# A transformer stack with cross-attention: heads in 32 rows of TensorE, and keys by way of DRAM

## The chip, the cores and the metric

One core of a Trainium2 chip runs the whole program as one launch. The metric is the device time of one execution in microseconds, as the median of several executions. TensorE multiplies, VectorE, ScalarE and GpSimd work elementwise, and SyncE issues the DMAs.

## The reference, cut to what matters

Eight layers work on `x`, 32 batches of 100 queries of 128 values, and each adds its gated result to `x`: attention, feed-forward, four times over. Three of the attention layers (called a0, a1 and a3 here) have 16 heads of 8 values and look at 1444 context rows of each batch:

```
q = layernorm(x) @ Wq;  k = ctx @ Wk;  v = ctx @ Wv           # per head: 8 of 128 columns
s = q @ k.T * scale                                           # 100 x 1444 for each of 16 heads
a1: s masked by a 0/1 mask [32, 100, 1444];  a3: keys from lens[b] on get -1.0e6
x += gate * (softmax(s) @ v) @ Wo
```

The fourth attention layer and the feed-forward layers are other functions.

## The kernel before, in words

`attention_phase` (line 195) is called three times: for a0, with a mask for a1 and with lengths for a3. Each call is one block in which five engines run their own lists of instructions and meet at semaphores. A batch's 16 heads are two halves of 8; the keys come in 12 tiles of 128 for scores and in 3 chunks of 480 or 482 for maxima. A batch is 24 units (`UNITS`). A unit has two maximum matmuls (`max_mm`, line 838), the scores of one half against one tile of 128 keys (`score_mm`, line 853), one exponential (`exps`, line 538), and its share of the product with the values (`pv_mm`, line 871), which is issued for two units together after each even unit. Maxima run ahead of scores by `LEAD` = 16 units, since a half's scores need its maxima.

Float32 accuracy is made from parts rounded to `F32R`: keys and queries are split into a high and a low part, and the three products high by high, low by high and high by low are rows of one matmul. For this `stack` (line 221) holds, for each group of four heads, 96 rows of keys (high, low, high, copied by twelve DMAs per batch in `stack_load`, line 373) and 32 rows of ones; `qblk` (line 225) holds, for each head, 96 query rows, zero outside of the head's own 8 (`q_spread`, line 439, on GpSimd), and 32 rows that carry the negated maxima (`neg_turn` on TensorE, `neg_copy` on VectorE, `neg_spread` on GpSimd). A maximum matmul therefore has 96 rows, 100 output rows and 480 or 482 columns. A score matmul has 128 rows, a stationary tile of 128 keys and 400 columns (four heads by 100 queries); two make a unit.

The maxima go through a ring of three PSUM banks (`RING`, line 191): `ring` (line 787) lets TensorE write a bank when what was in it three turns ago has been read. VectorE reduces each (`reduce_max`, line 649, with `tensor_reduce` in a0, and with a multiply or add of the mask or penalty in a1 and a3). The ring also takes each batch's other small products (`q_proj`, `u_proj`, `neg_turn`, `out_turn`, `concat_turn`, `out_proj`). Scores go through two slots of two banks (`slot`, line 792), which ScalarE empties; the projections `k_proj` and `v_proj` take the same slots. Which unit of a batch issues which of these is written out by hand in the constants of lines 295 to 297 and in the loop from line 925:

```
max_mm(2 * g)
score_mm(b, u)
# out_turn, concat_turn, out_proj, neg_turn, u_proj, q_proj at their units
max_mm(2 * g + 1)
# at even u: pv_mm of the two units before; then v_proj, k_proj at their units
```

In a1 `score_mm` adds a bf16 penalty matmul (line 867) to each of its two, and in a3 the penalty is the bias of the exponential (line 548).

## Time and profile before

| | us |
|---|---|
| median of 3 runs | 6736.84 (6734.98 to 6741.63) |
| profiled execution, its own time | 6736.52 |
| its span in the trace | 6734.7 |
| loop over batches in a0 (first to last score) | 1283.2, from 94.5 |
| loop over batches in a1 | 1718.3, from 2141.7 |
| loop over batches in a3 | 1351.6, from 5292.6 |
| TensorE, VectorE, ScalarE, GpSimd busy | 5947.1, 4732.6, 3471.3, 1972.7 |
| mean granted clock of TensorE | 0.938 |

The three loops are 4353.1 us of the span. Busy times of an engine merge instructions that overlap. A matmul of the trace lasts from its issue to its modelled end, so that many overlap; what one costs in a stream is the step from start to start. PE is TensorE's matmuls, PEld its loads of stationary operands, DVE is VectorE, ACT ScalarE, POOL GpSimd, SPq the DMA queue of SyncE.

### The profile page before, as it was taken

To read this page: it belongs to the slowest core of one execution; us is meant where nothing else is said; L and a number is where in the kernel's file an instruction comes from. 1 tells how busy PE (TensorE), PEld (TensorE's weight loads), DVE (VectorE), ACT (ScalarE), POOL (GpSimd) and SP (SyncE) were. 2 spreads that over 40 slices of the span, in tenths; PEclk is the share of its full clock that TensorE was granted. 3 is DMA by queue.
4 is the path that set the end of the run, shared out by engine and by line. 5 is a ranking of instruction groups with operands and counts; after the bars stand their busy time and mean duration, and the time that the engine had idled before them with its cause. 6 is when DMAs were issued, how large, how long until landed. Compare 5 with 4: busy or idle time off the path is not lost. (4 is left out here: it accounts for less than half of the span.)

```text
span 6734.7 us, 123692 instructions
## 1 busy us (share of the span) xinstructions
PE 5947.1 (88%) x42776; PEld 4044.1 (60%) x42776; DVE 4732.6 (70%) x12652; ACT 3471.3 (52%) x5250; POOL 1972.7 (29%) x1415
## 2 busy tenths in 40 slices
PE   6999999969897999999999956768498799999996
PEld 4666666659894555555555545645388466566653
DVE  6878777867676666666666676634577777777775
ACT  3666666655553444444444433423255466666664
POOL 2222222224453222222222122334255222222220
PEclk9999999989997999999999977878699799999998
DMA  3333333220002333333333132356332333232321
GB/s 75 77 78 73 72 72 75 63 68 21 21 21 68 81 77 81 78 79 75 76 79 75 35 68 52 60 157 183 98 118 81 82 72 71 67 69 68 69 67 25
DMA packets 200964, 492.88 MB, mean 73 GB/s; under 512 B 31689, under 2 KB 135318, under 8 KB 199162
## 3 DMA queue, kind: packets, MB, share of 16 engines
q1 hardware_dynamic: 200386, 485.47, 29.5%
q8 instruction: 327, 5.36, 0.3%
q14 instruction: 251, 2.06, 0.1%
HBM read 270.18 MB, written 2.25 MB: 40 GB/s over the span
## 5 line engine op out<-in xcount | busy, mean ns | idle before, releaser
L850 PE MATMUL a_max<-a_stack,a_qblk 96*100 96x482 f32 (+1 forms) x4608 | 2003.5, 455 | 114.3 <-DVE a_mx L671 35.7
L550 ACT ACTIVATE a_probs<-a_scores 128x800 f32<-128x800 f32 (+1 forms) x1536 | 1281.3, 838 | 1019.0 <-PE a_scores L867 656.9
L863 PE MATMUL a_scores<-a_qblk,a_stack 128*128 128x400 f32 (+1 forms) x4608 | 1378.7, 372 | 8.1 <-POOL a_qblk L455 2.7
L665 DVE CUSTOM_DVE_ANT_0 a_dump<-a_max,a_mqf 100x482 f32<-100x482 f32 (+1 forms) x1536 | 978.5, 657 | 426.4 <-PE a_max L850 395.6
L850 PEld LDWEIGHTS a_max<-a_stack,a_qblk 96*100 96x100 f32 x4608 | 767.2, 167 | 745.1 <-issue 205.6
L671 DVE CUSTOM_DVE_ANT_0 a_dump<-a_max,a_penq 100x482 f32<-100x482 f32 (+1 forms) x1536 | 955.6, 657 | 280.9 <-PE a_max L850 261.7
L657 DVE TENSOR_REDUCE a_mx<-a_max 100x1 f32<-100x482 f32 (+1 forms) x1536 | 941.4, 654 | 257.6 <-PE a_max L850 239.8
L879 PE MATMUL a_pv<-a_probs,a_v_aug 128*32 128x200 f32 x18432 | 1051.8, 340 | 3.4 <-ACT a_probs L548 2.1
L863 PEld LDWEIGHTS a_scores<-a_qblk,a_stack 128*128 128x128 f32 (+1 forms) x4608 | 840.4, 186 | 185.6 <-issue 52.7
L1165 POOL TENSOR_TENSOR f_hb<-f_hb,f_wb 128x400 f32<-128x400 f32 x560 | 655.8, 1185 | 965.1 <-DVE f_hb L1413 490.2
L548 ACT ACTIVATE a_probs<-a_scores,a_kbias 128x800 f32<-128x800 f32 (+1 forms) x768 | 697.5, 926 | 413.6 <-PE a_scores L863 413.4
L431 POOL TENSOR_TENSOR a_klo<-a_kf,a_khi 128x1444 fp32r<-128x1444 f32 x96 | 316.0, 3292 | 1511.0 <-ACT a_khi L511 1067.9
L879 PEld LDWEIGHTS a_pv<-a_probs,a_v_aug 128*32 128x32 f32 x18432 | 458.5, 108 | 475.5 <-issue 309.4
L455 POOL TENSOR_TENSOR a_qblk<-a_nsb,a_blk 32x800 fp32r<-32x800 f32 x192 | 292.4, 1523 | 1519.2 <-DVE a_nsb L697 1514.7
L1419 DVE TENSOR_TENSOR f_hl<-f_hb,f_hh 128x400 fp32r<-128x400 f32 x632 | 426.7, 675 | 248.3 <-ACT f_hh L1217 245.4
L1217 ACT ACTIVATE f_hh<-f_hb 128x400 fp32r<-128x400 f32 x632 | 339.9, 538 | 437.1 <-POOL f_hb L1165 399.7
L867 PE MATMUL a_scores<-a_pen,a_identb 128*128 128x400 bf16 (+1 forms) x1536 | 528.4, 344 | 0.0
L1497 PE MATMUL f_y<-f_hh,f_wd_lo 128*128 128x400 f32 x632 | 242.0, 383 | 217.9 <-DVE f_hl L1419 149.9
L445 POOL TENSOR_TENSOR a_qblk<-a_qs,a_blk 96x400 fp32r<-96x400 f32 x384 | 319.3, 851 | 87.9 <-PE a_scores L867 56.6
L1413 DVE TENSOR_TENSOR f_hb<-f_u,f_gs 128x400 f32<-128x400 f32 x496 | 281.7, 568 | 72.0 <-ACT f_gs L1229 67.8
L867 PEld LDWEIGHTS a_scores<-a_pen,a_identb 128*128 128x128 bf16 (+1 forms) x1536 | 147.0, 96 | 297.4 <-issue 296.6
L1229 ACT ACTIVATE f_gs<-f_g 128x400 f32<-128x400 f32 x496 | 247.8, 500 | 136.1 <-PE f_u L1499 128.3
(302 smaller groups left out, 8471.7 us busy)
## 6 DMA issues: line engine op xcount, KB each, us to landing
a_stack<-a_khi SPq DMA_DIRECT2D x768, 180.5 KB, 3.4
a_ctxT<-in_ctxT_dram SPq DMA_DIRECT2D x128, 722.0 KB, 8.5
a_stack<-a_klo SPq DMA_DIRECT2D x384, 180.5 KB, 3.5
f_wb<-weights_by_token SPq DMA_DIRECT2D x24, 1600.0 KB, 10.7
f_wb<-weights_by_token SPq DMA_DIRECT2D x64, 400.0 KB, 6.3
a_ctxn<-in_ctxn_dram SPq DMA_DIRECT2D x32, 704.0 KB
a_mt_i<-in_mask1T_dram SPq DMA_DIRECT2D x32, 600.0 KB, 6.9
a_mq_i<-in_mask_dram SPq DMA_DIRECT2D x32, 564.1 KB
```

Source lines behind the costliest of these rows:

```text
L548: act.activation(out_, in_, ACT.Exp, bias=kbias[0:rows, b:b + 1, kt], scale=scale).then_inc(sc_free, 1)
L550: act.activation(out_, in_, ACT.Exp, scale=scale).then_inc(sc_free, 1)
L657: nc.vector.tensor_reduce(out_, src, AX.X, ALU.max).then_inc(mx_free, 1)
L665: nc.vector.tensor_tensor_reduce(dump[:, k % 2, 0:n], src, mqf[:, b % 2, o:o + n], 1.0, -3.0e38, ALU.mult, ALU.max, out_).then_inc(mx_free, 1)
L671: nc.vector.tensor_tensor_reduce(dump[:, k % 2, 0:n], src, penq[:, b % 2, o:o + n], 1.0, -3.0e38, ALU.add, ALU.max, out_).then_inc(mx_free, 1)
L850: pe.matmul(to[0:S, 0:n], qblk[0:96, b % 2, HALF * h + head, :], stack[0:96, b % 2, g, o:o + n], start=True, stop=True).then_inc(mx_full, 1)
L863: ins = pe.matmul(out_, stack[:, b % 2, 2 * h + g, kt * D:kt * D + r], qblk[:, b % 2, HALF * h + 4 * g:HALF * h + 4 * g + 4, :].rearrange( ...
L867: ins = pe.matmul(out_.rearrange("p (h s) -> p h s", h=4), identb[0:r, 0:r], bc(pen[0:r, b % 2, kt, :], 1, 4), start=False, stop=True)
L879: ins = pe.matmul(p_pv[32 * t:32 * t + 32, 0:2 * S], v_aug[0:r, b % 2, kt, head:head + 2, :].rearrange("p h d -> p (h d)"), probs[0:r, u % ...
L1165: pool.tensor_tensor(hb[:, slot(n, c), :], hb[:, slot(n, c), :], wb[:, q, row, :], ALU.mult).then_inc(hw_ready, 1)
L1217: act.activation(hh[:, half(n, c), :], hb[:, slot(n, c), :], ACT.Copy).then_inc(hh_ready, 1)
L1419: nc.vector.tensor_tensor(hl[:, half(n, c), :], hb[:, slot(n, c), :], hh[:, half(n, c), :].bitcast(F32), ALU.subtract).then_inc(hl_ready, 1)
```

## The change

Each head gets 32 rows of its own: in `stack` and in the new `qst` (which replaces `qblk`, three batches deep) 8 rows carry ones against two rows of negated maximum (and in a3 a row of key penalties against a one), 24 carry the three products. Head 4r + g lies in rows 32r to 32r + 31 of group g. Maximum matmuls and score matmuls have 32 rows. A score matmul serves one head (100 columns), so that a unit has eight of them, two by two in different rows and different banks. `LEAD` becomes 24, and halves alternate (`half_of`), so that maxima and scores of one unit lie in different rows. A unit's order is: penalty (a1), maximum, four scores, maximum, four scores, then the other products. A maximum's VectorE instruction in a3 becomes the plain `tensor_reduce`, and its exponential has no bias. The high and low keys are stored to DRAM by two DMAs per batch and read back into `stack` by eight (twelve in a3). GpSimd makes `qst` in `q_parts` and the split maxima in `neg_parts`; `neg_turn` has four matmuls of 64 output rows per half; `neg_rows` on VectorE adds them into `qst`. In a0 and a3 `q_proj` adds a matmul of one row per group (bias, or the one against the penalty). Score tiles and penalties of the last key tile have 128 columns instead of 36. ScalarE's `q_round` is gone. The semaphore changes that follow from this are left out here.

```diff
-LEAD = 16
+LEAD = UNITS
+ROWS = 32
...
-        qblk = sb("qblk", [D, 2, HEADS, S], F32R)
+        qst = sb("qst", [D, 3, GROUPS, S], F32R)
...
-        OUT_AT, CONCAT_AT, WO_AT, NEG1_AT, U_AT, Q_AT, NEG0_AT = 2, 5, 8, 9, 13, 18, 21
-        V01_AT, V2_AT, K0_AT, K12_AT = 9, 11, 13, 15
-        K0_FIRST, K12_FIRST, Q_FIRST, NEG_FIRST = 5, 8, 11, 14
+        PARTS = 16 * (4 if lens is None else 6)
+        OUT_AT, NEG1_AT, CONCAT_AT, WO_AT, Q_AT, U_AT, NEG0_AT = 2, 4, 5, 8, 10, 13, 15
+        K0_AT, K12_AT, V01_AT, V2_AT = 1, 3, 7, 9
+        K0_FIRST, K12_FIRST, Q_FIRST, NEG_FIRST = 3, 6, 9, 14
...
+        def max_of(k):
+            b, at = divmod(k // 2, UNITS)
+            j, at = divmod(at, KT)
+            return b, j, at // NCH, at % NCH, k % 2
+        def half_of(b, j):
+            return (b + j) % 2
+        def scored(eng, b, j):
             if b >= 0:
-                full(eng, "exp", UNITS * b + KT * (h + 1) - 1)
+                full(eng, "exp", UNITS * b + KT * (j + 1) - 1)
+        def stack_there(eng, b, j):
+            eng.wait_ge(stack_in[b % 2][half_of(b, j)], (b // 2 + 1) * PARTS)
...
-            def stack_load(b, h):
+            def k_store(b):
                 sp.wait_ge(klo_ready, b + 1)
-                apart(sp, passed["sp"])
-                scored(sp, b - 2, h)
-                for g in (2 * h, 2 * h + 1):
-                    for part, src in enumerate((khi, klo, khi)):
-                        sp.dma_start(stack[32 * part:32 * part + 32, b % 2, g, :].bitcast(F32),
-                                     src[32 * g:32 * g + 32, :].bitcast(F32)).then_inc(stack_in[b % 2][h], 16)
+                if b >= SLOTS:
+                    stack_there(sp, b - SLOTS, 0)
+                    stack_there(sp, b - SLOTS, 1)
+                for part, src in enumerate((khi, klo)):
+                    sp.dma_start(k_dram[b % SLOTS, :, :, part, :, :], src[:, :].bitcast(F32)).then_inc(k_out, 16)
+            def stack_load(b, j):
+                h = half_of(b, j)
+                sp.wait_ge(k_out, 32 * (b + 1))
+                scored(sp, b - 2, j)
+                if lens is not None and b == 0:
+                    sp.wait_ge(gone_out, 16)
+                for r in (2 * h, 2 * h + 1):
+                    at, from_ = ROWS * r, k_dram[b % SLOTS, r]
+                    sp.dma_start(stack[at + 8:at + 24, b % 2, :, 0:KEYS].bitcast(F32),
+                                 from_.rearrange("g p i k -> (p i) g k")).then_inc(stack_in[b % 2][h], 16)
+                    sp.dma_start(stack[at + 24:at + 32, b % 2, :, 0:KEYS].bitcast(F32),
+                                 from_[:, 0].rearrange("g i k -> i g k")).then_inc(stack_in[b % 2][h], 16)
+                    if lens is not None:
+                        sp.dma_start(stack[at + 2:at + 3, b % 2, :, 0:KEYS].bitcast(F32),
+                                     gone_dram[b:b + 1, :].unsqueeze(1).broadcast_to([1, GROUPS, KEYS]))\
+                          .then_inc(stack_in[b % 2][h], 16)
...
+            def q_parts(b):
+                taken(pool, "q", b)
+                scored(pool, b - 3, 1)
+                step(pool.tensor_copy(qh[:, :, :], qf[:, :, :]))
+                step(pool.tensor_scalar(ql[:, :, :], qh[:, :, :].bitcast(F32), low[:, 0:1], None, ALU.mult))
+                pool.tensor_tensor(qst[:, b % 3, :, :], qf[:, :, :], ql[:, :, :], ALU.add).then_inc(qst_ready, 1)
+            def neg_parts(b, j):
+                h = half_of(b, j)
+                pool.wait_ge(nm_ready, 2 * b + j + 1)
+                if b > 0:
+                    full(pool, "neg", 2 * (b - 1) + 1 - j)
+                cols = nmsp[:, h, :, :].rearrange("p g (r w) -> p g r w", w=ROWS)
+                nm_ = nm[:, h, :].rearrange("p (g r) -> p g r", r=2)
+                step(pool.tensor_copy(cols[:, :, :, 0], nm_))
+                pool.tensor_tensor(cols[:, :, :, 1], nm_, cols[:, :, :, 0].bitcast(F32),
+                                   ALU.subtract).then_inc(negm_ready, 1)
...
+            def neg_rows(b, j):
+                full(dve, "neg", 2 * b + j)
+                at = 2 * ROWS * half_of(b, j)
+                q_ = qst[at:at + 2 * ROWS, b % 3, :, :]
+                nc.vector.tensor_tensor(
+                    q_, p_ring("neg", 2 * b + j)[at:at + 2 * ROWS, 0:GROUPS * S].rearrange("p (g s) -> p g s", g=GROUPS),
+                    q_.bitcast(F32), ALU.add).then_inc(mx_free, 1)
...
             def q_proj(b):
                 to = ring("q", b)
                 for g in range(GROUPS):
-                    ins = pe.matmul(to[0:96, g * S:(g + 1) * S], wq[:, g, :], xnT[:, b * S:(b + 1) * S],
-                                    start=True, stop=True)
+                    ins = pe.matmul(to[:, g * S:(g + 1) * S], wq[:, g, :], xnT[:, b * S:(b + 1) * S],
+                                    start=True, stop=q_row is None)
+                    if q_row is not None:
+                        ins = pe.matmul(to[:, g * S:(g + 1) * S], q_row[:, g, :], ones_row[:, :], start=False, stop=True)
                 ins.then_inc(mx_full, 1)
...
+            def neg_turn(b, j):
+                to = ring("neg", 2 * b + j)
+                h = half_of(b, j)
+                at = 2 * ROWS * h
+                pe.wait_ge(negm_ready, 2 * b + j + 1)
+                for g in range(GROUPS):
+                    ins = pe.matmul(to[at:at + 2 * ROWS, g * S:(g + 1) * S], nmsp[:, h, g, :].bitcast(F32),
+                                    ident[0:S, 0:S], start=True, stop=True)
+                ins.then_inc(mx_full, 1)
             def max_mm(k):
-                b, r = divmod(k, 2 * UNITS)
+                b, j, g, c, r = max_of(k)
                 if b >= B:
                     return
-                h, r = divmod(r, 2 * KT)
-                head, c = divmod(r, NCH)
                 o, n = CHUNKS[c]
-                if r == 0:
-                    pe.wait_ge(stack_in[b % 2][h], (b // 2 + 1) * 96)
-                    pe.wait_ge(qblk_ready, 2 * b + h + 1)
+                if k % (2 * KT) == 0:
+                    stack_there(pe, b, j)
+                    pe.wait_ge(qst_ready, b + 1)
                 to = ring("max", k)
-                g = 2 * h + head // 4
-                pe.matmul(to[0:S, 0:n], qblk[0:96, b % 2, HALF * h + head, :], stack[0:96, b % 2, g, o:o + n],
+                at = ROWS * (2 * half_of(b, j) + r)
+                pe.matmul(to[0:S, 0:n], qst[at:at + ROWS, b % 3, g, :], stack[at:at + ROWS, b % 2, g, o:o + n],
                           start=True, stop=True).then_inc(mx_full, 1)
-            def score_mm(b, u):
-                h, kt = divmod(u, KT)
-                r = D if kt < KT - 1 else LAST
-                if kt == 0:
-                    pe.wait_ge(qneg_ready, 2 * b + h + 1)
-                if u == 0 and mask is not None:
+            def score_mm(b, u, g):
+                j, kt = divmod(u, KT)
+                if u % KT == 0 and g == 0:
+                    taken(pe, "neg", 2 * b + j)
+                to = slot("exp", UNITS * b + u) if g == 0 and mask is None else p_slot("exp", UNITS * b + u)
+                for r in range(2):
+                    at = ROWS * (2 * half_of(b, j) + r)
+                    ins = pe.matmul(to[:, r, g * S:(g + 1) * S], stack[at:at + ROWS, b % 2, g, kt * D:(kt + 1) * D],
+                                    qst[at:at + ROWS, b % 3, g, :], start=mask is None,
+                                    stop=mask is None or g == GROUPS - 1)
+                if g == GROUPS - 1:
+                    ins.then_inc(sc_full, 1)
+            def penalty_mm(b, u):
+                if u == 0:
                     pe.wait_ge(pen_ready, b + 1)
                 to = slot("exp", UNITS * b + u)
-                for g in range(2):
-                    out_ = to[0:r, g, 0:4 * S]
-                    ins = pe.matmul(out_, stack[:, b % 2, 2 * h + g, kt * D:kt * D + r],
-                                    qblk[:, b % 2, HALF * h + 4 * g:HALF * h + 4 * g + 4, :].rearrange("p h s -> p (h s)"),
-                                    start=True, stop=mask is None)
-                    if mask is not None:
-                        ins = pe.matmul(out_.rearrange("p (h s) -> p h s", h=4), identb[0:r, 0:r],
-                                        bc(pen[0:r, b % 2, kt, :], 1, 4), start=False, stop=True)
-                ins.then_inc(sc_full, 1)
+                for i in range(2):
+                    pe.matmul(to[:, i, 0:4 * S].rearrange("p (h s) -> p h s", h=4), identb[:, :],
+                              bc(pen[:, b % 2, u % KT, :], 1, 4), start=True, stop=False)
...
                     g = UNITS * b + u + LEAD
+                    if mask is not None:
+                        penalty_mm(b, u)
                     max_mm(2 * g)
-                    score_mm(b, u)
+                    score_mm(b, u, 0)
+                    score_mm(b, u, 1)
+                    max_mm(2 * g + 1)
+                    score_mm(b, u, 2)
+                    score_mm(b, u, 3)
```

## Rows read from the trace of the kernel before

**Rows 1.** The page: busy us, share of the span and instructions of each engine
```profile
PE 5947.1 (88%) x42776; PEld 4044.1 (60%) x42776; DVE 4732.6 (70%) x12652; ACT 3471.3 (52%) x5250; POOL 1972.7 (29%) x1415
```

**Rows 2.** Three batch loops: stretch, us; PE, PEld, DVE, ACT, POOL busy; clock, DMA share, GB/s
```profile
94.50:1377.70 1283.20, 1277.14 (x10735) 825.66 (x10736) 1012.46 (x1972) 807.12 (x1073) 328.38 (x245) 1.00 0.31 71
2141.70:3860.00 1718.30, 1682.23 (x12953) 957.10 (x12953) 1156.35 (x3725) 842.49 (x1167) 426.94 (x276) 1.00 0.31 75
5292.60:6644.20 1351.60, 1297.42 (x10674) 810.15 (x10674) 1060.17 (x3507) 855.46 (x1074) 328.59 (x245) 1.00 0.30 68
```

**Rows 3.** The same view: maxima alone before the first loop, scores alone at its end
```profile
70.50:94.50 24.00, 20.12 (x49) 9.10 (x49) 21.41 (x38) 5.05 (x6) 7.45 (x5) 0.71 0.38 78
...
1361.50:1377.70 16.20, 15.62 (x164) 7.61 (x163) 1.37 (x6) 12.47 (x17) 1.52 (x1) 1.00 0.00 1
```

**Rows 4.** Timeline, two units of the first phase: start us, us, engine, line, instructions
```profile
699.47 0.65 DVE L657 TENSOR_REDUCE a_mx<-a_max 100x1 f32<-100x482 f32 x1
...
700.18 0.46 PE L850 MATMUL a_max<-a_stack,a_qblk 96*100 96x482 f32 x1
...
700.47 0.53 PE L863 MATMUL a_scores<-a_qblk,a_stack 128*128 128x400 f32 x2
...
700.66 0.16 PEld L850 LDWEIGHTS a_max<-a_stack,a_qblk 96*100 96x100 f32 x1
...
700.84 0.39 PE L850 MATMUL a_max<-a_stack,a_qblk 96*100 96x482 f32 x1
...
701.15 0.50 PEld L879 LDWEIGHTS a_pv<-a_probs,a_v_aug 128*32 128x32 f32 x16 [0.33 <-issue]
...
701.97 0.46 PE L850 MATMUL a_max<-a_stack,a_qblk 96*100 96x480 f32 x1
...
702.27 0.52 PE L863 MATMUL a_scores<-a_qblk,a_stack 128*36 128x400 f32 x2
...
702.47 2.37 DVE L657 TENSOR_REDUCE a_mx<-a_max 100x1 f32<-100x480 f32 x4 [0.23 <-PE a_max L850]
...
702.63 0.60 PE L850 MATMUL a_max<-a_stack,a_qblk 96*100 96x482 f32 x2
...
703.75 0.16 PEld L879 LDWEIGHTS a_pv<-a_probs,a_v_aug 128*32 128x32 f32 x8 [0.33 <-ACT a_probs L550]
```

**Rows 5.** Timeline, one unit of the masked phase and its projection of queries
```profile
3001.07 0.34 PE L867 MATMUL a_scores<-a_pen,a_identb 128*128 128x400 bf16 x1
...
3001.44 0.34 PE L867 MATMUL a_scores<-a_pen,a_identb 128*128 128x400 bf16 x1
...
3001.62 0.85 PE L817 MATMUL a_max<-xnT_a,a_wq 128*96 128x100 f32 x8
```

**Rows 6.** Timeline, TensorE in projections of values and keys
```profile
149.61 1.95 PE L810 MATMUL a_scores<-a_wv,a_ctxT 128*128 128x128 f32 x16
...
161.01 1.78 PE L803 MATMUL a_scores<-a_ctxT,a_wk 128*128 128x482 f32 x4
```

**Rows 7.** Timeline, TensorE beside a matmul of one row (line 904)
```profile
146.36 0.38 PE L902 MATMUL a_max<-a_wo,a_ctsb 128*100 128x128 f32 x2
...
146.67 0.25 PEld L904 LDWEIGHTS a_max<-a_bo,a_ones_row 1*100 1x100 f32 x2
...
146.67 0.46 PE L904 MATMUL a_max<-a_bo,a_ones_row 1*100 1x128 f32 x2
...
147.06 0.16 PEld L850 LDWEIGHTS a_max<-a_stack,a_qblk 96*100 96x100 f32 x1
```

**Rows 8.** Groups by line in the first loop: copy of the queries on VectorE
```profile
L634 DVE TENSOR_TENSOR a_qf<-a_max,a_bq 96x400 f32<-96x400 f32 x30 | 17.1, 571 | 1.5
```

**Rows 9.** Timeline ahead of the first maximum: first copy of keys, first maximum
```profile
62.94 0.62 SPq L379 DMA_DIRECT2D a_stack<-a_khi  x1
...
70.53 2.19 PE L850 MATMUL a_max<-a_stack,a_qblk 96*100 96x480 f32 x4 [9.26 <-DMA a_stack<-a_khi]
```

**Rows 10.** The page, DMA queue: packets, MB, share of 16 engines
```profile
q1 hardware_dynamic: 200386, 485.47, 29.5%
```

More of the change, by code:

```diff
@@ L575, in _ @@
             k_evac("k12", 1)
-            q_round(1)
             em_make(0, 0)
@@ L830, in u_proj @@
                 ins.then_inc(mx_full, 1)
-            def neg_turn(b, h):
-                to = ring("neg", 2 * b + h)
-                pe.wait_ge(negm_ready, 2 * b + h + 1)
-                pe.matmul(to[96:128, 0:S], nmsp[:, h, :].bitcast(F32), ident[0:S, 0:S],
-                          start=True, stop=True).then_inc(mx_full, 1)
+            def neg_turn(b, j):
+                to = ring("neg", 2 * b + j)
+                h = half_of(b, j)
+                at = 2 * ROWS * h
[4 more added lines that the diff above has]
+                ins.then_inc(mx_full, 1)
```

299 lines of the change are left out of this document (133 added, 166 removed).

## The prediction

> **What bounds the kernel now.** I read the page first: TensorE is the busiest engine, VectorE next [rows 1]. Busy shares over a whole program hide its stages, so I took each attention loop by itself [rows 2]. In a0 TensorE is busy 99.5% of 1283.2 us, in a1 97.9% of 1718.3, in a3 96.0% of 1351.6; VectorE is at 79, 67 and 78%, and ScalarE at 63% at most. The granted clock is 1.00 there. These loops, 4353.1 of 6734.7 us, are all that the change touches, with their starts. The last 16 units of a loop have no maxima and take 16.2 us [rows 3], so the other 752 of a0 take (1283.2 - 16.2)/752 = 1.685 us each, or 40.4 us a batch.
>
> Next the timeline of two units, for the steps in which TensorE streams [rows 4]. Two score matmuls in 0.53 us, the last 0.35 long: a step of 0.18. Two maxima in 0.60: 0.22. The product with the values, 16 matmuls, from 701.15 to 701.97: 0.81 for two units. From the maximum at 700.84 to 701.15 it is 0.31, and that step should be 0.22: about 0.10 us is lost when the engine turns from whole-array matmuls to those of 32 output rows. On the way back (701.97 to 702.27) a load of 0.08 stands open. The pair is 1.78 + 0.81 = 2.60 us, a batch 12 pairs = 31.2. VectorE's four reductions in 2.37 step by (2.37 - 0.65)/3 = 0.57, or 2.29 per pair.
>
> The rest of a batch is single products. Eight matmuls of q_proj in 0.85 us [rows 5] and sixteen of v_proj in 1.95 [rows 6], with the last of each at about 0.26 (two in 0.38 with a step of 0.11, [rows 7]), are steps of 0.086 and 0.112; four of k_proj in 1.78 [rows 6] step by about 0.40. So a batch has 6 x 0.40 + 24 x 0.112 + 8 x 0.086 = 5.8 us of these, and 2.4 us for neg_turn, out_turn, concat_turn and out_proj (my estimate from these steps). That makes 8.2, and 39.4 in all against 40.4 measured: the sum by steps holds, and 1.0 us a batch is waiting.
>
> **The score and maximum matmuls.** Columns per unit fall from 2 x 482 + 2 x 400 in a row to four streams side by side. The trace has no two matmuls in different rows, so this price is bounded. The nearest row is v_proj: a stationary load of 128 columns for every 128-column matmul, a step of 0.112, which the load sets, as it is the same for 96 columns at 0.086 [rows 5, 6]. Every score matmul has 100 columns (0.04 us of streaming) and a load of 128. If the two rows in use load side by side, a unit's four pairs of scores take 4 x 0.112 = 0.45 us and both maxima run beside them, against 0.80 before. That is the low end. The high end is everything in turn: eight loads (0.90) and two more of 0.08, 1.06 us. I take 0.45, since the product with the values does just this in columns: 16 loads in 0.50 us and four matmuls at a time [rows 4]. The Trainium skill says that tiles in different rows load and multiply in parallel, with 3.07 times the speed for four (TensorE: Matmul & The Clock Gate, Part 3); this trace doesn't show it.
>
> **Turning between forms.** Here is a price against the change. The matmul of one row in out_proj lies in the trace [rows 7]: two whole-array matmuls start at 146.36 and 146.47 and stream until 146.58, but the load for one row starts at 146.67; 0.09 is lost, and a load of 0.08 stands open; the way back costs it again. The Trainium skill has this as a rule (TensorEngine Tiling (Array Packing), Key Properties: a change of tiling mode drains the engine), and the trace agrees. Before, only the value products (and a few small ones) paid it. Now the scores and maxima are in the small form and every single product between them turns twice: 2 x 0.10 + 0.107 + 0.083 = 0.39. q_proj in a0 and a3 alternates between whole matmuls and one-row ones, four times there and back: 4 x (4 x 0.11 + 2 x 0.20) = 3.35 us a batch instead of 0.69.
>
> **The ring.** TensorE's part of a pair in a0 becomes 0.107 + 7 x 0.112 + 0.04 + 0.10 + 0.81 = 1.85 us, but VectorE needs 2.29, and the ring of three couples them. The pair's fourth maximum takes the bank of its first. The first starts, is reduced 0.50 later (701.97 to 702.47), the reduction takes 0.65, and the next maximum goes 0.06 after a reduction's end (699.47 + 0.65 to 700.18) [rows 4]: 1.20. Behind the fourth come two more score steps, streaming, the turn and the values: 1.20 + 0.107 + 0.11 + 0.14 + 0.82 = 2.4 us, against 2.60. All else queued on TensorE stands behind that wait.
>
> **Single products after.** At odd units they fall between the pair's second and third maximum, where 0.55 us of ring wait can hide them: k 0.81 and 1.62, v 1.79 and 0.90, neg 0.70 (eight matmuls now, by 0.09), concat 0.22: 6.0 us, plus six times (0.39 - 0.57): 5.0. At even units nothing hides: out 0.45, neg 0.70, out_proj 0.70, q_proj 3.35, four turns of 0.20, four ring waits of 0.20 (their bank is the pair's second, still unread), and 0.4 behind the normalisation: 7.2. The negated maxima hold VectorE for 0.5. A batch: 28.8 + 5.0 + 7.2 + 0.5 = 41.5 us, 1.73 a unit against 1.685.
>
> **VectorE, ScalarE, GpSimd.** neg_rows is an addition of 400 columns from PSUM, as q_bias is now at 0.57 [rows 8]; it can cost between nothing more than the small copy that it replaces and 0.57 more, and I take the whole 0.57, twice a batch. Two of three steps of each negation go to GpSimd. VectorE's sum stays about 1.3 us a unit. ScalarE loses q_round, and GpSimd the spreads; at 63 and 26% busy [rows 2] they set nothing. GpSimd's longest list, the low half of the keys and three steps on queries, is some 7 us by the widths, and what waits for it has 3 to 10 units.
>
> **Start and end.** 24 units of maxima go ahead instead of 16. The 16 took 24.0 us, held by VectorE [rows 3]; eight more at two reductions of 0.57 each are 9 us. The keys' way through DRAM puts a store before the load: now the first maximum comes 7.6 us after the first copy is issued (62.94 to 70.53) [rows 9]; a store in front adds between 3 and 15, and I take 7, one such passage. The last 24 units without maxima take about 25. Each phase: +16.
>
> **DMA.** Queue 1 moved 485.47 MB in 29.5% of 16 x 6734.7 us, 15.3 GB/s per engine [rows 10]. A batch now moves 2.2 MB for stack, 1.5 stored, 0.7 of context: 4.4 MB, or 18 us of 16 engines in 41. Cost zero: half a batch (12 units, 20 us) covers each load of 1.1 MB. If that cover fails, see the fourth rival.
>
> **The sum.** a0: 744 x 1.73 + 25 + 16 = 1328, +45. a3: out_proj has no bias, so 41.0 a batch, 1.71 a unit: 744 x 1.71 + 41 = 1313 against 1351.6, -38. (Its reductions lose the add and their second read.) a1: four penalties a pair by 0.18 (two steps, score and penalty, from 3001.07 to 3001.44 [rows 5]) make 3.33 before. After, each unit is 0.40 of penalties, turn 0.10, load 0.107, three steps 0.34, 0.14: 1.09; the pair 2.17 + 0.82 = 3.0, and the ring doesn't bind, since the fourth maximum comes at 1.4. Minus 0.33 x 12, plus 1.9 for neg, q and open loads: -2.1 a batch, -65; -6 at the tail, +16: -55. Together -48: the profiled execution's 6736.5 gives 6688, and the median shown is 0.3 above it. I say 6685.
>
> **Rivals.**
> (1) Faster: VectorE and the ring don't hold TensorE, so that its own time counts: 12 x 1.85, single products at odd units 6.0 + 6 x 0.39, at even units 5.2 + 4 x 0.20, so 36.6 us a batch, a0 -107, a3 -191, a1 -55: 6380. For it: VectorE has 20% idle [rows 2]. Against it: the 1.20 us above. 0.17.
> (2) Slower: different rows take turns. Place: every pair of score matmuls. If the loads queue, a unit is 1.06 and a pair 2 x 1.06 + 0.14 + 0.82 = 3.1, a batch 12 x 3.1 + 8.4 + 6.0 = 51.5: 2.15 a unit, a0 +375, a3 +290, a1 (0.6 us a unit more) +400: 7800. If only the streams do (402 + 336 ns of columns and ten times 0.015 between them, from the steps of 0.18 for 400 and 0.22 for 482), a unit is 0.88: 7400. It decides early: each 0.1 us a unit above 0.45 costs a1 77 us, and 0.06 or so eats the gain. For it: the trace shows no overlap by rows. 0.15.
> (3) Loads hide less: none runs behind a matmul in its own rows, so a step is 0.107 + 0.04 = 0.15. In before one does: the second score starts at 700.47 + 0.18, and the load for the next maximum, in rows that this score uses, at 700.66 [rows 4]. About +50 in a1, +40 in each other: 6810. The Trainium skill says that overlap needs different row groups (TensorE: Matmul & The Clock Gate, Part 3), and the trace disagrees. 0.04.
> (4) The stores use few of the 16 engines: 1.5 MB over four at 15.3 GB/s is 24 us a batch on these, with 16 to 18 of the rest, as much as the batch lasts, and the next load comes late. a0 and a3 +50 each: 6780. 0.06.
>
> **How the numbers follow.** My forecast has 0.58, with its own range 6550 to 6820. The full range leaves out (2) and the far part of (1): 6340 to 6960. About 0.2% can be told from no change. The forecast lies near zero, with 0.38 of its 0.58 below -0.2%, 0.06 within and 0.14 above; with (1) and a little of (4) faster is 0.56, same 0.06, slower 0.38.
>
> **What would show it.** Right: score matmuls in two rows starting within 0.02 us of each other, the next pair 0.11 later; a wait for a reduction ahead of the second maximum of even units; 0.1 us lost at each turn; a pair of 2.4 us in a0; a0 slower, a3 and a1 faster. Wrong: steps above 0.15; waits on stack's DMAs; a pair below 2.2 us; or a granted clock below 1.00 in a loop.

## The result, and the profile after

The changed kernel takes 7781.74 us (median of 4 runs, 7780.74 to 7807.54) against 6739.24 us for the kernel before on the same chip: a ratio of 1.155, 95% interval 1.153 to 1.158. It is 15.5% slower; the forecast was 6685 us.

The first view is the page of the changed kernel: each engine's busy us, the granted clock in 40 slices of the span, and the DMA queue.

```profile
PE 6851.8 (88%) x58264; PEld 4803.4 (62%) x58264; DVE 4620.9 (59%) x10700; ACT 3399.7 (44%) x5154; POOL 1605.0 (21%) x1415
...
PEclk7676666666999699989999978787995566666666
...
q1 hardware_dynamic: 219624, 630.31, 41.4%
```

TensorE is as busy as before in share [rows 1], but the row of the clock says something new: 6 in the slices of the first and last attention phase, 9 in the middle. The same three loops as in [rows 2], by stretches (us; busy time of PE, PEld, DVE, ACT, POOL; granted clock, DMA share, GB/s):

```profile
128.10:1853.60 1725.50, 1697.72 (x15960) 1129.23 (x15963) 997.36 (x1829) 803.79 (x1044) 206.99 (x244) 0.65 0.44 79
2645.90:4463.40 1817.50, 1665.86 (x17939) 1038.98 (x17939) 1089.92 (x3564) 836.68 (x1138) 307.46 (x275) 0.91 0.53 95
5926.00:7685.70 1759.70, 1739.35 (x15901) 1152.62 (x15901) 996.64 (x1829) 795.95 (x1044) 207.12 (x244) 0.62 0.44 79
```

With a0's and a3's loops 441 and 406 us longer than before (1284.7 and 1353.3 to the last product with the values) and a1's 98, the granted clock is 0.65, 0.62 and 0.91 where it was 1.00 in all three. TensorE is busy 98.4% of a0's loop: it doesn't wait, it runs slowly. The 0.65 is a mean of two levels, between which the clock goes in every batch:

```profile
195.00:215.00 20.00, 19.17 (x239) 13.98 (x238) 13.15 (x25) 11.79 (x16) 6.48 (x6) 1.00 0.47 132
216.00:252.00 36.00, 36.00 (x298) 22.39 (x290) 19.71 (x37) 15.80 (x20) 2.33 (x3) 0.50 0.41 50
253.00:269.00 16.00, 15.37 (x187) 11.20 (x188) 10.45 (x20) 8.46 (x12) 3.10 (x4) 1.00 0.55 160
```

All of the slow 36 us are busy. Ahead of the rise lies the projection of keys, on the whole array (244.35 to 247.87); ahead of the fall lie q_proj with its one-row matmuls (207.38 to 210.52) and plain pairs of 32-row work.

The stretches ahead of the first score are 34, 30 and 31 us longer. Here are those before a0's first maximum and from there to its first score, and a0's end, where no maxima are left:

```profile
62.00:85.80 23.80, 3.70 (x20) 3.51 (x19) 0.00 (x0) 1.69 (x3) 4.48 (x4) 0.57 0.78 130
85.80:128.10 42.30, 36.33 (x80) 16.25 (x80) 29.03 (x52) 4.52 (x5) 6.81 (x8) 0.54 0.63 92
1810.80:1853.60 42.80, 42.62 (x388) 28.93 (x389) 2.01 (x7) 19.49 (x24) 0.00 (x0) 0.50 0.00 1
```

The first maximum comes at 85.8 instead of 70.5 [rows 9], the maxima ahead take 42.3 us instead of 24.0 and the last 24 units 42.8 at a clock of 0.50 instead of some 25 [rows 3]. Part of the 42.3 is a wait: the first units' maxima want the second batch's keys, which come by way of DRAM too.

```profile
128.00 0.72 PE L874 MATMUL a_max<-a_stack,a_qst 32*100 32x480 f32 x1 [4.02 <-DMA a_stack<-a_k_parts]
```

Two pairs of units of a0, seen on TensorE, show what a lower clock does. First one that runs at full speed (start us, us, instructions):

```profile
211.34 0.46 PE L874 MATMUL a_max<-a_stack,a_qst 32*100 32x482 f32 x1
211.34 0.31 PE L884 MATMUL a_scores<-a_qst,a_stack 32*128 32x100 f32 x2
211.36 0.46 PE L874 MATMUL a_max<-a_stack,a_qst 32*100 32x482 f32 x1
...
212.55 0.46 PE L874 MATMUL a_max<-a_stack,a_qst 32*100 32x480 f32 x1 [0.30 <-DVE a_mx L680]
...
212.93 1.02 PE L907 MATMUL a_pv<-a_probs,a_v_aug 128*32 128x200 f32 x16
213.89 0.46 PE L874 MATMUL a_max<-a_stack,a_qst 32*100 32x482 f32 x1
```

Then one at half speed:

```profile
226.57 0.84 PE L884 MATMUL a_scores<-a_qst,a_stack 32*128 32x100 f32 x6
227.36 0.72 PE L874 MATMUL a_max<-a_stack,a_qst 32*100 32x482 f32 x1
...
228.00 1.56 PE L907 MATMUL a_pv<-a_probs,a_v_aug 128*32 128x200 f32 x16
229.50 0.72 PE L874 MATMUL a_max<-a_stack,a_qst 32*100 32x480 f32 x1
...
230.96 0.72 PE L874 MATMUL a_max<-a_stack,a_qst 32*100 32x482 f32 x1
```

Three things stand in these rows. Two maxima and two scores, in four different rows, start within 0.02 us (211.34 to 211.36): rows do run side by side. The full-speed pair takes 213.89 - 211.34 = 2.55 us, with 0.30 us of it a wait for a reduction ahead of its later maxima: that is the ring, where the prediction put it. And the other pair, 227.36 to 230.96, takes 3.60 us with the same instructions; no wait is left on TensorE. It is not twice 2.55 but near twice 1.85, the prediction's figure for TensorE's own part of a pair: at half speed the ring, which goes by VectorE, no longer holds TensorE back. The granted clock and the durations turn together: a maximum's 0.46 us becomes 0.69 at 215.10, and the view by stretches has 1.00 from 214 to 215 us, 0.58 in the next us and 0.50 in the one behind it.

a1 has a second loss, on none of the forecast's lists. All engines of one stall (idle time ahead and its releaser in brackets):

```profile
3004.05 3.27 POOL L480 TENSOR_TENSOR a_klo<-a_kf,a_khi 128x1444 fp32r<-128x1444 f32 x1 [9.35 <-ACT a_khi L548]
3007.29 3.25 POOL L508 TENSOR_SCALAR a_gone<-a_mt_i 128x1200 f32<-128x1200 int32 x1
...
3010.58 1.20 ACT L586 ACTIVATE a_pen<-a_gone 128x1200 bf16<-128x1200 f32 x1 [5.87 <-POOL a_gone L508]
3011.69 0.82 ACT L578 ACTIVATE a_probs<-a_scores 128x800 f32<-128x800 f32 x1
...
3012.56 0.89 PE L907 MATMUL a_pv<-a_probs,a_v_aug 128*32 128x200 f32 x8 [4.61 <-ACT a_probs L578]
```

GpSimd makes the low parts of the keys and then the mask; ScalarE stands in its queue at the penalty of the next batch (unit 5), which waits for that mask, with the exponentials behind it; TensorE waits 4.61 us for those. The view of waits has this one 31 times in the loop, 136.9 us in all:

```profile
PE a_pv L907 <- ACT a_probs L578: 136.9, 31, 4.6
```

Behind it the clock is down as well: the granted clock is 1.00 from 3000 to 3008 us and 0.50 from 3012.5 to 3018.

### The profile page after: what moved, and what is told of

Its sections match the earlier page's. It is cut to its first block and busy times, and to the rows that moved or that the text cites. A ratio compares the mean times of both kernels' runs of the same rounds, so it can differ in the third digit from the quotient of the medians.

```text
span 7778.9 us, 150520 instructions
## 1 busy us (share of the span) xinstructions
PE 6851.8 (88%) x58264; PEld 4803.4 (62%) x58264; DVE 4620.9 (59%) x10700; ACT 3399.7 (44%) x5154; POOL 1605.0 (21%) x1415
## 5 line engine op out<-in xcount | busy, mean ns | idle before, releaser
L578 ACT ACTIVATE a_probs<-a_scores 128x800 f32<-128x800 f32 (+1 forms) x2304 | 1930.9, 838 | 2208.8 <-PE a_scores L884 2207.7
L680 DVE TENSOR_REDUCE a_mx<-a_max 100x1 f32<-100x482 f32 (+1 forms) x3072 | 1852.6, 653 | 1259.5 <-PE a_max L874 1247.6
L884 PE MATMUL a_scores<-a_qst,a_stack 32*128 32x100 f32 x18432 | 1995.1, 348 | 0.0
L874 PE MATMUL a_max<-a_stack,a_qst 32*100 32x482 f32 (+1 forms) x4608 | 1664.4, 577 | 119.9 <-DMA a_stack<-a_k_parts 39.5
L884 PEld LDWEIGHTS a_scores<-a_qst,a_stack 32*128 32x128 f32 x18432 | 1651.4, 249 | 23.4 <-issue 13.3
L907 PE MATMUL a_pv<-a_probs,a_v_aug 128*32 128x200 f32 x18432 | 1443.5, 439 | 139.8 <-ACT a_probs L578 136.9
L874 PEld LDWEIGHTS a_max<-a_stack,a_qst 32*100 32x100 f32 x4608 | 598.6, 200 | 1125.0 <-DVE a_mx L680 468.1
L823 PE MATMUL a_scores<-a_ctxT,a_wk 128*128 128x482 f32 (+1 forms) x576 | 445.4, 902 | 61.7 <-DVE a_ones_row L641 30.4
L895 PE MATMUL a_scores<-a_pen,a_identb 128*128 128x400 bf16 x1536 | 416.4, 354 | 0.0
L830 PE MATMUL a_scores<-a_wv,a_ctxT 128*128 128x128 f32 x2304 | 383.7, 329 | 0.0
```

The lines of the kernel that those rows point to most:

```text
L578: act.activation(out_, in_, ACT.Exp, scale=scale).then_inc(sc_free, 1)
L680: nc.vector.tensor_reduce(out_, src, AX.X, ALU.max).then_inc(mx_free, 1)
L823: ins = pe.matmul(to[:, i, 0:n], wk[:, :], ctxT[:, b % 2, o:o + n], start=True, stop=True)
L830: ins = pe.matmul(to[:, i // 4, i % 4 * D:(i % 4 + 1) * D], ctxT[:, b % 2, o:o + D], wv[:, :], start=True, stop=True)
L874: pe.matmul(to[0:S, 0:n], qst[at:at + ROWS, b % 3, g, :], stack[at:at + ROWS, b % 2, g, o:o + n], start=True, stop=True).then_inc(mx_full, 1)
L884: ins = pe.matmul(to[:, r, g * S:(g + 1) * S], stack[at:at + ROWS, b % 2, g, kt * D:(kt + 1) * D], qst[at:at + ROWS, b % 3, g, :], start=m ...
```

## The experiments

Theory A: TensorE's granted clock falls because the 32-row matmuls leave most of the array at rest, though the engine is never idle; a1 is spared since its penalty runs on the whole array in every unit. The rivals are that the clock falls for another reason (theory B, and A2 for one such: the cadence of short matmuls with a load before each), that rows don't run side by side, and that the loss is one of waits. From fill1 to pen_rows each run is one profiled execution, and the kernel before took 6726 to 6754 us beside them; hybrid's total is a median of five, and its loops are from one of them.

Loops whose code is the same differ between such runs. a0's takes 1725.5, 1716.0 and 1673.5 us in after, pen_late and pen_rows, and a1's 1817.5, 1845.9 and 1862.9 in after, fill1 and fill2. So some 50 us in one loop can't be told from nothing where the clock is well below 1.00, nor some 20 where it is near (a1 in pen_late, combo, fill_rows, fill_part and hybrid: 1578.8 to 1600.6).

| run | total us | a0 loop us, clock | a1 loop us, clock | a3 loop us, clock |
|---|---|---|---|---|
| before | 6736.5 | 1284.7, 1.00 | 1719.8, 1.00 | 1353.3, 1.00 |
| after | 7781.0 | 1725.5, 0.65 | 1817.5, 0.91 | 1759.7, 0.62 |
| fill1 | 7548.9 | 1595.3, 0.85 | 1845.9, 0.90 | 1632.1, 0.81 |
| fill2 | 7875.1 | 1737.7, 0.84 | 1862.9, 0.89 | 1800.0, 0.79 |
| b_cols | 7360.7 | 1622.3, 0.99 | 1720.1, 1.00 | 1627.8, 0.99 |
| b_rows | 7715.9 | 1634.1, 0.94 | 1991.5, 0.98 | 1713.9, 0.90 |
| q_dve | 7495.0 | 1670.8, 0.64 | 1816.0, 0.91 | 1540.6, 0.71 |
| pen_late | 7529.9 | 1716.0, 0.66 | 1582.2, 0.98 | 1759.1, 0.62 |
| combo | 6798.6 | 1380.2, 0.97 | 1586.6, 0.98 | 1357.8, 0.97 |
| rows_same | 9478.9 | 2356.6, 0.58 | 2269.6, 0.83 | 2382.1, 0.57 |
| fill_rows | 6963.7 | 1392.3, 0.85 | 1594.6, 0.98 | 1498.8, 0.76 |
| fill_part | 6844.7 | 1392.4, 0.91 | 1600.6, 0.97 | 1375.5, 0.90 |
| pen_rows | 7425.7 | 1673.5, 0.68 | 1510.5, 0.90 | 1768.7, 0.62 |
| hybrid | 6618.5 | 1285.7, 1.00 | 1578.8, 0.99 | 1348.7, 1.00 |

**Added work on the whole array (fill1, fill2).** In a0 and a3, ahead of a unit's maxima and scores; the scores overwrite what it leaves. `fillw` and `fillx` are ones.

```diff
+            def filler_mm(b, u):
+                to = slot("exp", UNITS * b + u)
+                for i in range(2):                      # range(1) in fill1
+                    pe.matmul(to[:, i, 0:4 * S], fillw[:, :], fillx[:, :], start=True, stop=True)
```

> The changed kernel with two more whole-array matmuls of 400 bf16 columns in every unit of a0 and a3, into the banks that the scores then overwrite, as a1's penalty has them. Theory A (the matmuls of 32 rows with 100 columns leave TensorE so little at work that the granted clock falls to 0.5, and a1 escapes it because its penalty runs on the whole array in every unit): the clock in the loops of a0 and a3 rises from 0.65 and 0.62 to 0.9 or more, as in a1, and although 0.4 us of work is added per unit (9.6 us a batch at full clock), a0 falls from 1724 us to 1550 to 1650. Theory B (the clock is set by something else in a0 and a3, waits or a state of the chip): the clock stays near 0.65 and a0 grows by 0.4 to 0.8 us a unit, to 2030 or more.

> As the run with two added whole-array matmuls per unit, with one (0.17 us a unit at full clock). Theory A: the clock lies between that of the changed kernel (0.65) and that of the run with two; if one is enough to hold it at full, a0 takes 1450 to 1550 us, the best of the three; if not, it stays near 1700. Theory B: clock 0.65, a0 about 1880.

More work made the kernel faster. With one added matmul a unit a0's loop falls by 130 us and a3's by 128, and the clock goes from 0.65 and 0.62 to 0.85 and 0.81. The rows of a0's loop in the view by stretches, of fill1 and then of fill2:

```profile
128.30:1723.60 1595.30, 1575.90 (x16729) 1003.38 (x16730) 998.64 (x1829) 804.42 (x1044) 207.20 (x244) 0.85 0.48 85
```
```profile
127.40:1865.10 1737.70, 1728.50 (x17497) 1024.19 (x17497) 1000.04 (x1829) 804.05 (x1044) 207.46 (x244) 0.84 0.44 78
```

Theory B is out: it had a0 at about 1880 us in fill1. But theory A's numbers don't hold either: the second matmul raises the clock no further and costs 142 us, or 0.185 a unit, about its own step of 0.18; neither run gets to 0.9, and a0 is at 1595 where 1450 to 1550 was expected.

In fill1's a0 the clock falls 12 times, 9 of them during q_proj, whose products alternate with the one-row matmuls. Here are the stretches on both sides of one such fall; its q_proj goes from 731.57 to 735.36.

```profile
716.00:733.00 17.00, 16.74 (x182) 11.62 (x178) 10.86 (x19) 10.18 (x13) 3.26 (x1) 1.00 0.48 115
734.00:777.00 43.00, 43.00 (x339) 24.98 (x338) 21.87 (x40) 15.26 (x20) 3.64 (x7) 0.50 0.41 57
```

**Cadence or form (b_cols, b_rows), in the kernel before.** One cuts the scores, the other takes rows from the maxima.

```diff
+                    if mask is None:                    # b_cols
+                        for i in range(4):
+                            ins = pe.matmul(to[0:r, g, i * S:(i + 1) * S], stack[:, b % 2, 2 * h + g, kt * D:kt * D + r],
+                                            qblk[:, b % 2, HALF * h + 4 * g + i, :], start=True, stop=True)
+                        continue
```
```diff
-                pe.matmul(to[0:S, 0:n], qblk[0:96, b % 2, HALF * h + head, :], stack[0:96, b % 2, g, o:o + n],
+                pe.matmul(to[0:S, 0:n], qblk[0:32, b % 2, HALF * h + head, :], stack[0:32, b % 2, g, o:o + n],
```

> The kernel before, with the two 400-column score matmuls of a unit in a0 and a3 cut into eight of 100 columns, whole array as before (a1 unchanged). It has the cadence of the new scores (a load of 128 columns for every 100 streamed) without their 32-row form. Step 0.11 instead of 0.18 per 400: 0.88 us a unit instead of 0.36, so at full clock a0 goes from 1283 to about 1680 and a3 from 1352 to about 1745, 7530 in all. Theory A1 (the form of 32 rows pulls the clock down, not the cadence): the granted clock stays 1.00 and these times hold. Theory A2 (the cadence does it, since TensorE is mostly loading): the clock falls below 0.9 in a0 and a3, and a0 takes 2000 or more.

> The kernel before, with its maxima over 32 rows of stack instead of 96 (the low parts are left out of the maxima), same columns and same order; the scores stay on the whole array. Per unit two turns between forms more each way, about 0.2 to 0.35 us: at full clock a0 about 1450 to 1550, the whole 7100 to 7450. Theory A1: with whole-array scores of 400 columns and values still there the clock stays above 0.9 or falls somewhat; whatever it does falls in a0 and a3 first and less in a1. Rival (any regular use of 32-row tiles pulls it down): the clock falls to 0.7 or less and a0 takes over 1700.

The loops of a0 in b_cols, then in b_rows:

```profile
96.30:1718.60 1622.30, 1621.86 (x15356) 1250.83 (x15360) 1085.40 (x1972) 818.01 (x1074) 326.58 (x245) 0.99 0.25 57
```
```profile
95.90:1730.00 1634.10, 1629.35 (x10752) 815.72 (x10752) 1077.20 (x1972) 813.16 (x1074) 326.78 (x245) 0.94 0.25 56
```

Eight whole-array matmuls of 100 columns a unit, each behind a load of 128, leave the clock at 0.99: the cadence alone isn't the cause. A unit costs 0.44 us more, less than the 0.52 expected (a0 1622 us instead of about 1680). Taking 64 of 96 rows from the maxima, with every count of instructions and columns kept, brings it to 0.94 and 0.90: the form moves it, or the turns between forms that come with it (fill_rows, below, parts the two). Most of b_rows' 349 us in a0 (0.45 a unit) is not the clock, though; it is these turns, in its timeline:

```profile
701.20 0.45 PE L850 MATMUL a_max<-a_stack,a_qblk 32*100 32x482 f32 x1
701.58 0.63 PE L863 MATMUL a_scores<-a_qblk,a_stack 128*128 128x400 f32 x2
702.14 0.46 PE L850 MATMUL a_max<-a_stack,a_qblk 32*100 32x482 f32 x1
```

A maximum and the scores take 701.20 to 702.14 = 0.94 us where the steps 0.22 and 2 x 0.18 [rows 4] make 0.58: two turns, 0.18 each with the open load, as forecast (0.10 and 0.08). They make 0.36 of the 0.45 a unit. The run's own expectation was too low: a0 at 1634 us instead of 1450 to 1550, the whole at 7716 instead of 7100 to 7450.

**The one-row matmuls (q_dve).** `q_copy` becomes an addition of the bias on VectorE, and q_proj has no second matmul.

```diff
-                    if q_row is not None:
-                        ins = pe.matmul(to[:, g * S:(g + 1) * S], q_row[:, g, :], ones_row[:, :], start=False, stop=True)
```
```diff
+                    nc.vector.tensor_tensor(qf[:, :, :], src, bc(q_row[:, :], 2, S), ALU.add).then_inc(mx_free, 1)
```

> The changed kernel without the one-row matmuls of q_proj in a0 and a3: the same numbers are added by VectorE as it takes the queries from PSUM (a copy of 400 columns becomes an addition). At full clock TensorE's q_proj shrinks from 3.1 us to 0.85, 2.3 us a batch, 70 us in each of a0 and a3, in line with the 2.66 that the prediction put on it. Theory A (activity of the whole array decides the clock, and a q_proj that turns back and forth for 3 us is a gap in it): more than the 70 us each, with the granted clock above 0.65 and 0.62. Theory A' (the one-row matmuls are only a cost of their own): 7640 us, and the clock as it was.

In the changed kernel's timeline q_proj alternates between the forms every 0.39 us:

```profile
207.38 0.47 PE L837 MATMUL a_max<-xnT_a,a_wq 128*128 128x100 f32 x2
207.78 0.46 PE L840 MATMUL a_max<-a_ones_row,a_q_row 1*128 1x100 f32 x2
208.17 0.47 PE L837 MATMUL a_max<-xnT_a,a_wq 128*128 128x100 f32 x2
...
210.13 0.46 PE L840 MATMUL a_max<-a_ones_row,a_q_row 1*128 1x100 f32 x2
210.52 0.89 PE L907 MATMUL a_pv<-a_probs,a_v_aug 128*32 128x200 f32 x16
```

210.52 - 207.38 = 3.14 us, against 3.35 forecast. Without them a0 gains 55 us at an unchanged clock (0.64); a3 gains 219, with the clock at 0.71. a3 goes with theory A. a0's 55 us would fit A', their own cost, but they are no more than a0's loop differs by with this code unchanged (1673.5 us in pen_rows), so a0 decides nothing. Why its clock stays is open.

**a1's stall (pen_late).**

```diff
-                    if u == 5 and b + 1 < B:
+                    if u == 12 and b + 1 < B:
                         pen_make(b + 1)
```

> The changed kernel with ScalarE's making of a1's penalty moved from unit 5 of the batch before to unit 12; nothing else is touched. The trace of the changed kernel shows TensorE waiting 4.6 us for the exponentials once in each batch of a1, ScalarE for the masks, which GpSimd makes behind the keys' low parts. If that stall is a1's loss, its loop falls by 30 batches of 4.6 us, from 1817 to about 1680 us, and the whole to 7640; a0 and a3 stay. Rival: the stall also gives TensorE no penalty for its clock, or what it hides comes due elsewhere in the batch (the clock's low stretch in a1, the ring), and a1 gains less than 70 us.

a1's loop falls by 235 us, 1.7 times what its waits add up to and 98 more than expected. The stall is gone (TensorE is idle for over 1 us once in the loop, where it was 32 times), and so is most of the clock's loss: 0.98 instead of 0.91. In the changed kernel a maximum takes 0.45 us ahead of the stall shown above (at 3005.04) and 0.72 behind it (at 3014.16). The loop is now 138 us faster than that of before.

```profile
2636.50:4218.70 1582.20, 1566.91 (x17939) 976.74 (x17939) 1089.63 (x3564) 829.60 (x1138) 307.73 (x275) 0.98 0.61 109
```

**All three (combo).** fill1, q_dve and pen_late in one kernel.

> One added whole-array matmul per unit in a0 and a3, the query bias on VectorE, and a1's penalty made at unit 12, together. In the run with one added matmul a batch at full clock took 44.0 us and the clock fell behind a q_proj with one-row matmuls. Theory A: without these it stays near 1.00, a batch takes 44.0 - 2.3 = 41.7 us, a0 and a3 about 1310 to 1350 us, a1 about 1680, the whole about 6850. Rival: one added matmul isn't enough by itself, the clock stays at 0.85 and a0 about 1520, the whole 7250.

```profile
128.40:1508.60 1380.20, 1357.89 (x16490) 880.37 (x16490) 993.20 (x1829) 803.60 (x1044) 206.92 (x244) 0.97 0.55 98
...
5348.60:6706.40 1357.80, 1337.29 (x16427) 868.42 (x16428) 991.24 (x1829) 793.27 (x1044) 206.96 (x244) 0.97 0.57 102
```

a0 and a3 lose 345 and 402 us, in a0 far more than the parts (130 + 55), in a3 hardly more than loops of one code differ by (128 + 219). The clock no longer falls at q_proj, as it did in fill1: the added matmul holds it once q_proj has no one-row matmuls. By its timeline (starts of scores at 700.51 and 742.49, 24 units apart) a batch at full clock takes 42.0 us. a0 is 30 us above its expected range all the same. The whole, 6798.6 against 6733.9, is 1.0% slower than the kernel before.

**Side by side or in turn (rows_same).** The second head's scores come from the first one's rows.

```diff
-                    at = ROWS * (2 * half_of(b, j) + r)
+                    at = ROWS * 2 * half_of(b, j)
```

> The changed kernel with both heads' score matmuls of a pair in the same 32 rows (the second head gets the first one's scores). If matmuls in different rows really load and stream side by side, this takes that away: a unit's scores need eight loads in turn instead of four pairs, 0.86 us instead of 0.45 at full clock and twice that at half, so a0 grows by 0.3 to 0.8 us a unit, to 1950 to 2350, and a1 to 2100 or more. If side by side brings nothing (rows take turns anyway, my second rival), the times stay at 7780.

a0 grows by 631 us, 0.82 a unit, and a1 by 452; the prices behind the expectation were 0.41 a unit at full clock and 0.82 at half. The clock falls too (0.65 to 0.58 and 0.91 to 0.83), and its part isn't separated. That rows run side by side, and that it pays, is shown; the second rival is refuted.

**The added matmul's form and place (fill_rows, fill_part), in combo.**

```diff
-                    pe.matmul(to[:, i, 0:4 * S], fillw[:, :], fillx[:, :], start=True, stop=True)
+                    at = 2 * ROWS * half_of(b, u // KT)
+                    pe.matmul(to[:, i, 0:4 * S], fillw[at:at + ROWS, :], fillx[at:at + ROWS, :], start=True, stop=True)
```
```diff
-                    else:
+                    elif u >= 10:
                         filler_mm(b, u)
```

> The combined kernel (one added matmul per unit, query bias on VectorE, a1's penalty at unit 12), with the added matmul of 400 bf16 columns on 32 rows instead of 128: same place, same columns, same time of its own. Theory A (what counts is work on the whole array) expects the clock of a0 and a3 to fall from 0.97 to 0.75 or less, near the 0.64 and 0.71 of the run without an added matmul, and a0 to rise from 1380 us to over 1600. Rival (any stream that fills the gaps between the loads holds the clock): clock 0.97 and a0 within 30 us of 1380.

> The combined kernel with its added matmul in units 10 to 23 of a batch only; the projections of keys and values (units 1 to 9) and the products turning the output are whole-array work of their own. Theory A: they are enough in those units, the clock stays near 0.97, and a0 and a3 lose 0.1 to 0.2 us in each of ten units a batch, 30 to 60 us each: 6700 to 6740 in all. Rival: the activity of these units isn't enough, the clock falls there, and a0 goes above 1400.

On 32 rows the same matmul leaves the clock at 0.85 and 0.76 instead of 0.97 and 0.97, a3 141 us slower. So rows count. And it isn't the turns that lower the clock: fill_rows has fewer of them than combo. But the 32-row matmul isn't worth nothing: without any added matmul the clock was 0.64 and 0.71 (q_dve), though in a3 0.05 is little. And a0 is only 12 us slower, because a 32-row matmul needs no turn and runs beside the maxima (both start at 751.16): its batches at full speed take 38.4 us (scores at 749.95 and 788.30) with a pair of 2.41, against 42.0 and 2.68 (760.85 to 763.53) in combo:

```profile
749.95 0.42 PE L891 MATMUL a_scores<-a_qst,a_stack 32*128 32x100 f32 x4
750.33 0.89 PE L920 MATMUL a_pv<-a_probs,a_v_aug 128*32 128x200 f32 x16
751.16 0.34 PE L901 MATMUL a_scores<-a_fillx,a_fillw 32*128 32x400 bf16 x1
751.16 0.45 PE L881 MATMUL a_max<-a_stack,a_qst 32*100 32x482 f32 x1
...
752.37 0.42 PE L891 MATMUL a_scores<-a_qst,a_stack 32*128 32x100 f32 x4
```

My expectation of over 1600 us missed that. fill_part went to the rival, though a0 stayed just below its 1400 us: with the added matmul left out of units 0 to 9 the clock is 0.91 and 0.90, so the whole-array work that is left there doesn't hold it. a0 and a3 are 12 and 18 us slower, which is no more than loops of one code differ by; it is the clock that tells.

**The penalty's form (pen_rows), in pen_late.**

```diff
-                    pe.matmul(to[:, i, 0:4 * S].rearrange("p (h s) -> p h s", h=4), identb[:, :],
-                              bc(pen[:, b % 2, u % KT, :], 1, 4), start=True, stop=False)
+                    at = ROWS * (2 * half_of(b, u // KT) + i)
+                    pe.matmul(to[:, i, 0:4 * S].rearrange("p (h s) -> p h s", h=4), identb[at:at + ROWS, :],
+                              bc(pen[at:at + ROWS, b % 2, u % KT, :], 1, 4), start=True, stop=False)
```

> The changed kernel with a1's penalty made at unit 12, and its penalty matmuls (bf16, 400 columns) on 32 rows in place of 128, so that only 32 keys of each tile get a penalty. Nothing else differs from the run with the penalty at unit 12 alone, whose a1 loop took 1582 us at a granted clock of 0.98. If the whole-array penalty is what kept a1's clock, a1 now falls to 0.65 to 0.85, as a0 does with and without an added 32-row matmul (0.85 and 0.64), and its loop takes over 1700 us, though a 32-row matmul saves the turns between forms. Rival (a1's clock has another reason, its waits or its u_proj): 0.95 or more, and 1500 to 1580 us.

```profile
2593.80:4104.30 1510.50, 1415.31 (x17939) 1009.94 (x17939) 1094.84 (x3564) 826.49 (x1138) 307.95 (x275) 0.90 0.64 114
```

Split: the clock falls, 0.98 to 0.90, but less than I said, and the loop is 72 us shorter, as the rival had it: the penalties need no turn now and start beside the maxima.

```profile
3102.03 0.34 PE L896 MATMUL a_scores<-a_pen,a_identb 32*128 32x400 bf16 x2
3102.03 0.45 PE L874 MATMUL a_max<-a_stack,a_qst 32*100 32x482 f32 x1
```

The whole-array penalty is part of what keeps a1's clock, not all.

**The form where it pays (hybrid).** a0 and a3 as before, a1 in the new form with its penalty at unit 12.

```diff
-            w = {k: A["a1_" + k] for k in ("wq", "wk", "wv", "wo")} | {"blk": A["blk"]}
-            attention_phase(nc, "a1", x, xnT, ident, w, dram, D ** -0.5, gates[0:S, 1:2], mask=(A["mask1"], A["mask1T"]))
+            w = {k: A["a1_" + k] for k in ("wq", "wk", "wv", "wo")} | {"low": A["low"]}
+            attention_rows(nc, "a1", x, xnT, ident, w, dram, D ** -0.5, gates[0:S, 1:2], mask=(A["mask1"], A["mask1T"]))
```

> The kernel before, with the 32-row form in a1 alone, where the penalty's whole-array matmuls hold the clock, and a1's penalty made at unit 12. If the parts add up, a1's loop takes 1582 us instead of 1720, its start and end cost 35 more, and the whole is 6734 - 138 + 35 = 6630 us, 1.5% faster than before. If the clock in a1 needs what goes ahead of it, or the start costs more than 100 us, nothing is gained.

```profile
94.30:1380.00 1285.70, 1279.09 (x10748) 826.47 (x10752) 1013.28 (x1972) 807.91 (x1074) 328.71 (x245) 1.00 0.31 71
2169.30:3748.10 1578.80, 1560.52 (x17935) 973.25 (x17939) 1090.64 (x3564) 829.50 (x1138) 307.90 (x275) 0.99 0.61 109
5173.50:6522.20 1348.70, 1297.34 (x10686) 810.62 (x10690) 1059.91 (x3507) 857.82 (x1075) 329.05 (x245) 1.00 0.30 68
```

6618.54 us (median of 5) against 6747.18 (median of 9): a ratio of 0.982, interval 0.980 to 0.983. It beats the kernel before by 1.8% and the changed one by 15%.

## Why the prediction was wrong

**The step that failed** is one that isn't worked out anywhere: every row behind the sum was read where "the granted clock is 1.00", and every price was carried over at that clock. "A granted clock below 1.00 in a loop" stood only among the things that would show it wrong, with no rival and no chance. In its place the runs showed a0 at 0.65: a pair of 3.60 us instead of 2.55, and a batch of 52.2 us (the same unit's scores start at 181.76 and 234.00) instead of 41.5. a0 came out at +474 (first maximum 15 later, the rest 459), a3 at +438 with the stretch ahead of it, against +45 and -38. Work in the form of 32 rows, without enough whole-array work beside it, doesn't hold the clock, as fill1, combo and fill_rows show. The closest row was [rows 3], where the clock is 0.71 while maxima alone run at the start; I used its times and passed over its clock.

A rule misled here. TensorE's busy share was read as its health, and the Trainium skill (TensorE: Matmul & The Clock Gate, Part 1) also ties the clock to how busy TensorE is and speaks of idle stretches as what lowers it. On idle stretches this case's trace agrees: behind a1's stall of 4.61 us the clock is at 0.50. For a busy engine it disagrees: at 98.4% busy the clock is 0.65, while added whole-array work raises it.

**a1** was forecast at -55 and came out at +127. The step that failed is "what waits for it has 3 to 10 units" for GpSimd's list: the list now starts with the low parts of the keys, and the mask behind them (3.25 us) is what ScalarE's queue stands for. I had counted who waits for the queries, not for the mask, nor what is queued behind that wait. With the wait taken away the loop is 138 us faster than before: the steps were right and if anything cautious (plain pairs of 3.0 us in pen_late, as forecast).

**What held, at full clock.** Side by side: starts within 0.02 us, a step of 0.11 from one pair of scores to the next (0.21 at half speed), and rows_same; rival (2) falls. The ring: a pair of 2.55 with a wait of 0.30 against 2.4 and 0.20; rival (1) falls. The turns: 0.18 in b_rows. q_proj: 3.14 against 3.35. A batch: combo's 42.0 us, which has 24 added matmuls and their turns and no one-row matmuls; fill_rows' 38.4, without these turns too, lies at the forecast's 41.5 - 2.66 = 38.8. DMA: TensorE waits for the stack's loads once in each phase, at the head of the loop (4.0, 4.7 and 5.3 us), and not in the batches behind it; rival (4) falls. Rival (3) had every step at 0.15. At full clock only a unit's first step is (211.34 to 211.49); the steps behind it are 0.11, so it falls too.

**Start and end** were +16 and measured 34 (15 ahead of the first maximum, 18 to the first score), with another 18 at the end, at a clock of 0.50 to 0.57. The store and load through DRAM added 15 instead of 7. Of the 18 to the first score, 9 are the additional maxima, as forecast; 4.0 are the wait for the second batch's keys, which the prediction had nowhere; q_proj takes 4.3 us (101.87 to 106.12) at the low clock, and the rest is not taken apart. The sum's last step is also 3 us off: 6736.5 - 48 + 0.3 gives 6689 and not 6685, which changes nothing.

What stays open: why one small change moves a3's clock and not a0's (q_dve), and how the rows, columns and loads of an instruction weigh against each other. The runs show only that work in the form of 32 rows doesn't hold the clock as whole-array matmuls do.

## What to carry to other kernels

Splitting matmuls into row tiles can bring what it promises in steps and still lose, if the engine then runs at 1.2 instead of 2.4 GHz; ask of every form what it leaves of the granted clock, and use it where whole-array work stays in every unit. When a busy engine slows down, look at the row of the clock before any wait. When one engine's list is reordered, follow each item to whoever waits for it and to what is queued behind that wait.
